# Two pieces of work change places in a software-pipelined attention layer: the block sums of the norms on TensorE, the sums of squares on GpSimd

## The chip, the cores and the metric

The kernel runs on one core of one Trainium2 chip. The metric is the device time of one execution in microseconds (us). Profiled times come from one execution that the hardware profiler recorded. The core has five engines with a queue each: TensorE (PE, with its weight loads shown apart as PEld), VectorE (DVE), ScalarE (ACT), GpSimd (POOL) and SyncE (SP), which here only issues DMAs. Each engine runs its queue strictly in order; between engines only semaphores order the work.

## The reference

The input x is 8 x 256 x 128. It is layer-normalised; then two branches are added to it. The first is causal attention with 16 heads of 64. The second is six layers of local attention and an MLP, and nearly all of the time is spent there:

```
for i in range(DEPTH):                                  # DEPTH = 6
    x = attn_layer(shift_tokens(x), ...) + x
    x = ffn_layer(shift_tokens(x), ...) + x

qkv = x @ Wqkv
q = l2norm(q) * qs ; k = l2norm(k) * ksc                # norm over the 64 elements of a head
q = q * cos * scale + rotate_half(q) * sin * scale      # k likewise, with 1 / scale
sim = q k^T * 8 in windows of 32 queries and 64 keys, softmax, times v, then @ Wo

a, gate = split(layernorm(x) @ W1 + b1)
out = a * gelu(gate) @ W2 + b2
```

## The kernel before

A *unit* is one batch element in one layer (6 x 8 = 48 units), a *group* is four heads of it, so there are 192 groups. After the causal branch the kernel runs a stream of *slots*; slot s works on five groups at different stages. Every engine has its own function `slot(s)`, and the statements in it are that engine's queue: the order is written out by hand, and the scheduler of the hardware changes nothing in it.

What a slot s does, along the chain of one group m:

- TensorE projects k and q of group s+4 in high and low parts (L789 to L791, `project`) and v (L799 to L801, `values`) into the banks B_K, B_Q and B_N.
- VectorE multiplies k and q with the rotary tables (L1025, L1026, `rotate`); ScalarE squares them (L520, `squares`); GpSimd adds the two halves of the rotated vectors (L395, `rotated`) and the two halves of the squares (L415, tile `sqs`).
- TensorE adds up `sqs` over the 32 rows of each head with a matrix of ones (L833, `con("blk")`, into B_N, semaphore `n_done`): these are the **block sums of the norms**. ScalarE turns them into 1/norm with Ln and Exp (L556, L559), VectorE bounds that (L1066, `bound_ready`), and GpSimd multiplies it into k and then q (L409, tile `z_norm`, `zn_ready`): the **normalisations**. SP copies the result into `zqk` with eight DMAs (L325). All of this is for group s+3.
- TensorE computes the scores of group s (L749, L758, `windows`), VectorE and ScalarE do the softmax (L1004, L1006, L552, L1011 to L1016).
- For group s-1 TensorE turns the probabilities (L768, `turn_windows`, into B_T, `turned`), ScalarE spreads them out (L539, `spread_ready`), TensorE multiplies them with V (L780, `weigh_windows`, 64 rows wide, into B_T again, `lpv_done`), and ScalarE copies the product to `yt` (L583, `lyt_ready`). `turn_windows` of the next slot waits for `lyt_ready`, since it writes B_T.
- For group s-2 TensorE multiplies `yt` with Wo (L828).
- In seven of eight slots there is also a piece of the MLP or of its layer norm: the gate product (L850, copied by ScalarE at L589), the up product (L864, taken by VectorE at L1085), the down product (L872), the centring (L886) and the mean of squares (L894) at the end of TensorE's slot. They all use the one bank B_M, so L886 and L894 wait for `gate_ready` or `hid_ready`, that is, until L589 or L1085 of the same slot has read it.

ScalarE's queue in a slot is: copy of v (L531), spreading (L539), in every fourth slot the layer norm's Ln and Exp (L546, L549), Exp of the scores (L552), Ln and Exp of the norms (L556, L559), squares of k (L520), the square or the scaling of the layer norm (L574 or L578), the copy to `yt` (L583), the gate (L589), once in eight slots the Gelu with its two table loads (L593, L595, L599, L542), squares of q (L520).

GpSimd's queue in a slot is: rotated k (two of L395), both normalisations (two of L409), sums of squares (L415), rotated q (two of L395); at the turn of a layer the split of the weights (L386, L388).

TensorE's queue in a slot, where the change is (before):

```
if two:
    pe.wait_ge(S["lv_ready"], s + 4)
    pe.wait_ge(S["sums_ready"], s + 4)
    pe.matmul(B_N[:, :], con("blk"), sqs...).then_inc(S["n_done"], 1)
if four:
    weigh_windows(s - 1, ...)
```

Of the kernel before, what the change touches and what calls it, by code (L numbers as in the profile page):

```python
# [11 lines left out]
ALU = mybir.AluOpType  # L12
# [4 lines left out]
P = 128  # L17
NB, T = 8, 256
# [3 lines left out]
G, HG = 4, 4  # L22
# [82 lines left out]
def build(nc, x, w_kv_down, w_kv_up, w_q, w_out, Wqkv, q_scale, k_scale, Wo, ln_g, ln_b, W1, b1, W2, b2, const, out):  # L105
    with ExitStack() as ctx:  # L106
        def sb(name, shape, dt=F32):
            return ctx.enter_context(nc.sbuf_tensor(name, shape, dt))

        def sem(name):  # L110
            return ctx.enter_context(nc.semaphore(name))
# [3 lines left out]
        def con(name):  # L115
            at, n = CONST[name]
            return consts[:, at:at + n]
# [32 lines left out]
        z_raw = sb("z_raw", [P, 2, 2, 2, T])  # L150
        z_norm = sb("z_norm", [P, 2, 2, 2, T])
# [14 lines left out]
        rinv = probs_t.rearrange("p h c -> p (h c)")[:, 2 * GW * 2:].rearrange("p (a t) -> p a t", a=2)  # L166
# [30 lines left out]
        S = {n: sem(n) for n in names}  # L197
# [3 lines left out]
        def after(eng, name, value):  # L201

            if not (isinstance(value, int) and value <= 0):
                eng.wait_ge(S[name], value)
# [31 lines left out]
        def stream(slot):  # L236

            for s in range(FIRST, LAST):
                slot(s)

        def active(s, first, last):

            return first <= s < last
# [5 lines left out]
        def layer_begun(s, at):  # L249

            l, k = divmod(s - at, LAYER)
            return l + 1 if k == 0 and 0 <= l < DEPTH - 1 else 0
# [118 lines left out]
        @block.gpsimd  # L371
        def _(pool):
            pool.memset(tiny[:, 0:1], 2.0 ** -64).then_inc(S["tiny_ready"], 1)
            pool.wait_ge(S["tiny_ready"], 1)
            pool.memset(tiny[:, 1:2], EPS).then_inc(S["tiny_ready"], 1)
            pool.wait_ge(S["tiny_ready"], 2)
            pool.memset(xs[64:P, :, 0:1], 0.0).then_inc(S["zeros_ready"], 1)
            pool.wait_ge(S["zeros_ready"], 1)
            pool.memset(par_rows[:, :], 0.0).then_inc(S["zeros_ready"], 1)

            pool.memset(v_late[0:WIN, :, 0, :], 0.0).then_inc(S["spread_zero"], 1)

            def split_weights(l, g):

                cols = slice(g * GW, (g + 1) * GW)
                pool.tensor_copy(w_high[:, :, cols], w_qkv[:, :, cols]).then_inc(S["split_high"], 1)  # L386
                pool.wait_ge(S["split_high"], G * l + g + 1)
                pool.tensor_tensor(w_low[:, :, cols], w_qkv[:, :, cols], w_high[:, :, cols].bitcast(F32), ALU.subtract).then_inc(S["split_done"], 1)  # L388

            def rotated(m, parity, idx, prod, mark):  # L390

                pool.wait_ge(S[prod], m + 1)
                after(pool, "zn_ready", m - 1)
                for half in range(2):
                    a = pool.tensor_tensor(z_raw[:, parity, idx, half, :], rot_u[:, idx, half, :], rot_v[:, idx, 1 - half, :], ALU.add)  # L395
                a.then_inc(S[mark], 1)

            def slot(s):
                one, two = active(s, -4, GROUPS - 4), active(s, -3, GROUPS - 3)
                if one:  # L400
                    rotated(s + 4, s % 2, 1, "k_prod", "k_summed")
                if two:

                    m, parity = s + 3, (s + 3) % 2
                    pool.wait_ge(S["bound_ready"], m + 1)
                    after(pool, f"z_in{(s + 1) % G}", 16 * 2 * HG * ((s + 1) // G + 1))
                    for idx, summed in ((1, "k_summed"), (0, "q_summed")):
                        pool.wait_ge(S[summed], m + 1)
                        a = pool.tensor_tensor(z_norm[:, parity, idx, :, :], rinv[:, idx, :].unsqueeze(1).broadcast_to([P, 2, T]), z_raw[:, parity, idx, :, :], ALU.mult)  # L409
                    a.then_inc(S["zn_ready"], 1)  # L410
                if one:
                    pool.wait_ge(S["k_square"], s + 5)
                    pool.wait_ge(S["q_square"], s + 5)
                    after(pool, "n_done", s + 4)
                    pool.tensor_tensor(sqs[:, :, :], sq[:, :, 0, :], sq[:, :, 1, :], ALU.add).then_inc(S["sums_ready"], 1)  # L415
                    rotated(s + 4, s % 2, 0, "q_prod", "q_summed")
                for g in range(G):
                    l = layer_begun(s, LAYER - 7 + g)
                    if l:
                        pool.wait_ge(S["w_in"], 16 * 3 * (l + 1))  # L420
                        pool.wait_ge(S["lv_done"], s + 4)
                        split_weights(l, g)

            pool.wait_ge(S["pv_done"], STEPS)
            pool.memset(spread[:, :, :, :], 0.0).then_inc(S["spread_zero"], 1)  # L425
            pool.wait_ge(S["w_in"], 16 * 3)
            for g in range(G):
                split_weights(0, g)
            stream(slot)

        @block.scalar
# [189 lines left out]
        def _(pe):  # L621
# [5 lines left out]
            for p in range(PAIRS):  # L627
                for k in range(2 * TT):
                    m = pe.transpose(bank[p][:, k * P:(k + 1) * P], xn_rows[:, 2 * TT * p + k, :], ident)
# [141 lines left out]
            def weigh_windows(n, unit, g, odd):  # L771

                pe.wait_ge(S["lv_ready"], n + 1)
                pe.wait_ge(S[f"v_late_in{g}"], 32 * (unit + 1))
                pe.wait_ge(S["spread_ready"], n + 1)
                for pair, tile, a in itertools.product(range(2), range(TILES), range(2)):
                    h, t = 2 * pair + a, tile // 2
                    f = slice(g * GW + h * D, g * GW + (h + 1) * D)
                    y = B_T[D * a:D * a + D, T * pair:T * pair + T].rearrange("p (t x s c) -> p t s x c", t=TT, x=2, s=2)
                    mm = pe.matmul(y[:, t, tile % 2, :, :], (v_sb if tile % 2 else v_late)[:, odd, t, f], spread[:, h, tile, :], start=True, stop=True,  # L780
                                   tile_position=(0, D * a), skip_group_check=True)
                mm.then_inc(S["lpv_done"], 1)
# [21 lines left out]
            def slot(s):  # L804
                g = s % G
                one, two = active(s, -4, GROUPS - 4), active(s, -3, GROUPS - 3)
                four = active(s, 1, GROUPS + 1)
# [11 lines left out]
                if active(s, 2, GROUPS + 2):  # L819

                    n, og, unit = s - 2, (s - 2) % G, (s - 2) // G
                    pe.wait_ge(S["lyt_ready"], n + 1)
                    if (s - 2) % LAYER < G:
                        pe.wait_ge(S[f"wo_in{og}"], 16 * ((s - 2) // LAYER + 1))
                    if og == 0:
                        after(pe, "lres_done", unit)
                    for c in (2 * og, 2 * og + 1):
                        mm = pe.matmul(B_X[:, 0:T], wo[:, c, :], yt[:, c, :], start=(c == 0), stop=(c == HD // P - 1))  # L828
                    mm.then_inc(S["lwo_done"], 1)
                if two:  # L830
                    pe.wait_ge(S["lv_ready"], s + 4)
                    pe.wait_ge(S["sums_ready"], s + 4)
                    pe.matmul(B_N[:, :], con("blk"), sqs[:, :, :].rearrange("p a t -> p (a t)"), start=True, stop=True).then_inc(S["n_done"], 1)  # L833
                if four:
                    weigh_windows(s - 1, (s - 1) // G, (s - 1) % G, (s - 1) // G % 2)
                for c in range(3):
                    if mlp_slot(s, 13 + c):
                        p = (s - 13 - c) // (2 * G)
# [67 lines left out]
            for h in range(HG):  # L906
                pt_taken(STEPS - 1, h)
            stream(slot)
            for p in range(PAIRS):
                pe.wait_ge(S["fin_sum"], p + 1)  # L910
                for k in range(2 * TT):
                    m = pe.transpose(bank[p][:, k * P:(k + 1) * P], xh[:, 2 * p + k // 2, (k % 2) * P:(k % 2 + 1) * P], ident)
# [225 lines left out]
```

## Time and profile before

| | us |
|---|---|
| median of 3 runs | 2024.2 |
| lowest, highest | 2021.36, 2025.51 |
| profiled execution, its own time | 2020.56 |
| its span in the profile | 2018.7 |
| granted TensorE clock, mean | 0.99 of full speed |

The span runs from the first to the last instruction of the program. Busy time of an engine is time in which it executes; an engine that waits for a semaphore is idle, and a row then names in brackets how long it sat and who released it. Matmuls are pipelined, so one row's end lies slightly behind the next row's start; distances are best taken from start to start. A slot is counted here from the start of `turn_windows` (L768) to the next one. The stream repeats itself every eight slots (two units), to within some hundredths of a microsecond; slot 0 to slot 7 below are the eight of one such group of eight, beginning with a slot whose number is divisible by eight.

### The profile page before, as it was taken

How to read it: one execution, taken by the hardware profiler on the slowest of the kernel's cores; microseconds unless marked ns; L12 is line 12 of the kernel's file. 1: busy time of each engine (PE TensorE's matmuls, PEld its weight loads, DVE VectorE, ACT ScalarE, POOL GpSimd, SP SyncE). 2: the span in 40 equal slices, each digit the busy share in tenths (PEclk: the TensorE clock that was granted, in tenths of full speed). 3: DMA queues.
4: the chain of work that ended last, by engine and by line, in shares of the span. 5: the costliest groups of instructions: out<-in, count | busy, mean ns of one | idle time of the engine just before them, and what ended most of it. 6: DMA issues, size and time to landing. Idle time of an engine off the chain costs nothing. (4 is left out here: it accounts for less than half of the span.)

```text
span 2018.7 us, 68336 instructions
## 1 busy us (share of the span) xinstructions
PE 1892.6 (94%) x26905; PEld 1389.3 (69%) x26905; DVE 1573.9 (78%) x3055; ACT 1407.2 (70%) x2840; POOL 1340.6 (66%) x1402
## 2 busy tenths in 40 slices
PE   4999997799999999999999999999999999999995
PEld 3677665677767777767777677776777776777762
DVE  5666665688888788888888888888878888888773
ACT  2666565578677767777777777768777777777762
POOL 0000002898898787897787987779878889787740
PEclk9999999999999999999999999999999999999996
DMA  3000000344434334333344343343333433333330
GB/s 97 2 1 0 0 6 30 97 108 106 124 86 104 96 100 127 87 95 97 99 113 111 85 105 95 100 124 88 100 97 99 128 88 94 97 99 101 93 92 21
DMA packets 190580, 171.18 MB, mean 85 GB/s; under 512 B 32160, under 2 KB 186440, under 8 KB 190152
## 3 DMA queue, kind: packets, MB, share of 16 engines
q1 hardware_dynamic: 190280, 167.02, 31.6%
q8 instruction: 208, 3.41, 0.7%
q14 instruction: 92, 0.75, 0.1%
HBM read 21.14 MB, written 1.05 MB: 11 GB/s over the span
## 5 line engine op out<-in xcount | busy, mean ns | idle before, releaser
L395 POOL TENSOR_TENSOR z_raw<-rot_u,rot_v 128x256 f32<-128x256 f32 x768 | 551.7, 741 | 151.9 <-DVE rot_v L1026 150.0
L409 POOL TENSOR_TENSOR z_norm<-probs_t,z_raw 128x512 f32<-128x512 f32 x384 | 492.7, 1304 | 97.5 <-DVE probs_t L1066 97.5
L1025 DVE TENSOR_TENSOR rot_u<-bank,tabs 128x512 f32<-128x512 f32 x384 | 262.7, 684 | 183.9 <-ACT sq L520 179.9
L789 PE MATMUL bank<-x_high,w_high 128*128 128x256 f32 x768 | 302.9, 394 | 2.3 <-issue 1.1
L1026 DVE TENSOR_TENSOR rot_v<-bank,tabs 128x512 f32<-128x512 f32 x384 | 260.9, 680 | 0.0
L552 ACT ACTIVATE pair_bank<-pair_bank 128x512 f32<-128x512 f32 x192 | 111.7, 582 | 211.3 <-DVE pair_bank L1006 211.0
L415 POOL TENSOR_TENSOR sqs<-sq 128x512 f32<-128x512 f32 x192 | 244.9, 1276 | 20.4 <-POOL z_norm L409 20.4
L520 ACT ACTIVATE sq<-bank 128x512 f32<-128x512 f32 x384 | 225.1, 588 | 47.8 <-PE bank L791 44.5
L780 PEld LDWEIGHTS bank<-probs_t,v_late 128*64 128x64 f32 x3072 | 155.2, 137 | 144.5 <-issue 144.5
L833 PE MATMUL bank<-sqs,consts 128*128 128x512 f32 x384 | 203.9, 613 | 52.5 <-POOL sqs L415 48.8
L539 ACT ACTIVATE probs_t<-bank 64x512 f32<-64x512 f32 x384 | 226.6, 590 | 33.8 <-PE bank L768 31.5
L425 POOL MEMSET probs_t<- 128x1024 f32 x1 | 1.0, 961 | 334.8 <-PE bank L690 334.8
L790 PE MATMUL bank<-x_high,w_low 128*128 128x256 f32 x768 | 216.5, 282 | 0.0
L791 PE MATMUL bank<-x_low,w_high 128*128 128x256 f32 x768 | 216.4, 282 | 0.0
L556 ACT ACTIVATE probs<-bank,tiny 128x512 f32<-128x512 f32 x192 | 131.9, 687 | 112.5 <-PE bank L833 111.5
L780 PE MATMUL bank<-probs_t,v_late 128*64 128x64 f32 x3072 | 199.1, 228 | 0.5 <-ACT probs_t L539 0.5
L828 PE MATMUL bank<-yt,wo 128*128 128x256 f32 x768 | 197.7, 380 | 1.3 <-ACT yt L583 1.3
L780 PE MATMUL bank<-probs_t,v_sb 128*64 128x64 f32 x3072 | 190.0, 222 | 0.0
L789 PEld LDWEIGHTS bank<-x_high,w_high 128*128 128x128 f32 x768 | 145.1, 189 | 62.2 <-issue 42.8
L790 PEld LDWEIGHTS bank<-x_high,w_low 128*128 128x128 f32 x768 | 145.7, 190 | 37.9 <-issue 37.9
L1004 DVE TENSOR_REDUCE nm<-pair_bank 128x8 f32<-128x512 f32 x192 | 131.9, 687 | 43.0 <-PE pair_bank L758 40.5
L758 PE MATMUL pair_bank<-zqk 64*32 64x64 f32 (+1 forms) x12288 | 162.2, 221 | 0.0
(154 smaller groups left out, 4507.9 us busy)
## 6 DMA issues: line engine op xcount, KB each, us to landing
zqk<-z_norm SPq DMA_DIRECT2D x1536, 64.0 KB, 2.1
v_late<-v_sb SPq DMA_DIRECT2D x192, 192.0 KB, 2.6
w_qkv<-in_L_ffn_Wqkv SPq DMA_DIRECT2D x18, 512.0 KB, 5.2
v_late<-v_sb SPq DMA_DIRECT2D x192, 32.0 KB, 2.2
wo<-in_L_ffn_Wo SPq DMA_DIRECT2D x24, 128.0 KB, 2.4
w<-in_L_ffn_W SPq DMA_DIRECT2D x12, 170.5 KB, 2.9
consts<-in_constants SPq DMA_DIRECT2D x1, 1088.0 KB, 5.2
w_qkv<-in_L_attn_w_kv_up SPq DMA_DIRECT2D x2, 512.0 KB, 6.3
```

What stands on the lines that cost most here:

```text
L395: a = pool.tensor_tensor(z_raw[:, parity, idx, half, :], rot_u[:, idx, half, :], rot_v[:, idx, 1 - half, :], ALU.add)
L409: a = pool.tensor_tensor(z_norm[:, parity, idx, :, :], rinv[:, idx, :].unsqueeze(1).broadcast_to([P, 2, T]), z_raw[:, parity, idx, :, :], ...
L415: pool.tensor_tensor(sqs[:, :, :], sq[:, :, 0, :], sq[:, :, 1, :], ALU.add).then_inc(S["sums_ready"], 1)
L520: act.activation(sq[:, idx, :, :], src[:, :].rearrange("p (a t) -> p a t", a=2), ACT.Square).then_inc(S[mark], 1)
L539: a = act.activation(spread[rows, :, :, WIN * x:WIN * x + WIN], tiles[rows, :, :, :], ACT.Copy)
L780: mm = pe.matmul(y[:, t, tile % 2, :, :], (v_sb if tile % 2 else v_late)[:, odd, t, f], spread[:, h, tile, :], start=True, stop=True, tile ...
L789: pe.matmul(dst, w_high[:, j, cols], x_high[:, odd, :], start=True, stop=False)
L790: pe.matmul(dst, w_low[:, j, cols], x_high[:, odd, :], start=False, stop=False)
L791: mm = pe.matmul(dst, w_high[:, j, cols], x_low[:, odd, :], start=False, stop=True)
L833: pe.matmul(B_N[:, :], con("blk"), sqs[:, :, :].rearrange("p a t -> p (a t)"), start=True, stop=True).then_inc(S["n_done"], 1)
L1025: dve.tensor_tensor(rot_u[:, idx, :, :], src, tabs[:, 2 * idx, :, :], ALU.mult)
L1026: dve.tensor_tensor(rot_v[:, idx, :, :], src, tabs[:, 2 * idx + 1, :, :], ALU.mult).then_inc(S[mark], 1)
```

## The change

On TensorE `weigh_windows` of group s-1 is issued in front of the block sums instead of behind them. On GpSimd the sums of squares are issued between the normalisation of k and that of q instead of behind both. Nothing is added or taken away.

```
@@ gpsimd
+            def normalise(parity, idx):
+
+                return pool.tensor_tensor(z_norm[:, parity, idx, :, :], rinv[:, idx, :].unsqueeze(1).broadcast_to([P, 2, T]), z_raw[:, parity, idx, :, :], ALU.mult)
...
                 if two:
 
-                    m, parity = s + 3, (s + 3) % 2
-                    pool.wait_ge(S["bound_ready"], m + 1)
+                    pool.wait_ge(S["bound_ready"], s + 4)
                     after(pool, f"z_in{(s + 1) % G}", 16 * 2 * HG * ((s + 1) // G + 1))
-                    for idx, summed in ((1, "k_summed"), (0, "q_summed")):
-                        pool.wait_ge(S[summed], m + 1)
-                        a = pool.tensor_tensor(z_norm[:, parity, idx, :, :], rinv[:, idx, :].unsqueeze(1).broadcast_to([P, 2, T]), z_raw[:, parity, idx, :, :], ALU.mult)
-                    a.then_inc(S["zn_ready"], 1)
+                    pool.wait_ge(S["k_summed"], s + 4)
+                    normalise((s + 3) % 2, 1)
                 if one:
                     pool.wait_ge(S["k_square"], s + 5)
                     pool.wait_ge(S["q_square"], s + 5)
                     after(pool, "n_done", s + 4)
                     pool.tensor_tensor(sqs[:, :, :], sq[:, :, 0, :], sq[:, :, 1, :], ALU.add).then_inc(S["sums_ready"], 1)
+                if two:
+                    pool.wait_ge(S["q_summed"], s + 4)
+                    normalise((s + 3) % 2, 0).then_inc(S["zn_ready"], 1)
+                if one:
                     rotated(s + 4, s % 2, 0, "q_prod", "q_summed")
@@ tensor
+                if four:
+                    weigh_windows(s - 1, (s - 1) // G, (s - 1) % G, (s - 1) // G % 2)
                 if two:
                     pe.wait_ge(S["lv_ready"], s + 4)
                     pe.wait_ge(S["sums_ready"], s + 4)
                     pe.matmul(B_N[:, :], con("blk"), sqs[:, :, :].rearrange("p a t -> p (a t)"), start=True, stop=True).then_inc(S["n_done"], 1)
-                if four:
-                    weigh_windows(s - 1, (s - 1) // G, (s - 1) % G, (s - 1) // G % 2)
```

TensorE's queue in a slot 2, before: the output product, the block sums, the products with V (their first three rows), the MLP's product, then, further on, the values, the centring and the next slot's turning.

```order
L828 MATMUL bank<-yt,wo 128x256
L833 MATMUL bank<-sqs,consts 128x512 [waits sums_ready,lv_ready]
L780 MATMUL bank<-probs_t,v_late 64x2x32 [waits spread_ready,v_late_in1,lv_ready]
L780 MATMUL bank<-probs_t,v_late 64x2x32
L780 MATMUL bank<-probs_t,v_sb 64x2x32 x2
...
L864 MATMUL bank<-xh,w 128x512 [waits hid_ready]
...
L799 MATMUL bank<-w_high,x_high 128x256 [waits ln_done]
...
L886 MATMUL bank<-xs,consts 128x256 [waits hid_ready,ln_var,lres_done]
L768 MATMUL bank<-consts,probs 128x128 [waits lyt_ready,weights_ready]
```

The same place of the changed kernel (its line numbers are 5 to 7 higher here):

```order
L833 MATMUL bank<-yt,wo 128x256
L785 MATMUL bank<-probs_t,v_late 64x2x32 [waits spread_ready,v_late_in1,lv_ready]
L785 MATMUL bank<-probs_t,v_late 64x2x32
L785 MATMUL bank<-probs_t,v_sb 64x2x32 x2
...
L840 MATMUL bank<-sqs,consts 128x512 [waits sums_ready,lv_ready]
L869 MATMUL bank<-xh,w 128x512 [waits hid_ready]
...
L804 MATMUL bank<-w_high,x_high 128x256 [waits ln_done]
...
L891 MATMUL bank<-xs,consts 128x256 [waits hid_ready,ln_var,lres_done]
L773 MATMUL bank<-consts,probs 128x128 [waits lyt_ready,weights_ready]
```

The block sums moved behind all sixteen products with V; each kept its waits, and what follows them stayed where it was.

GpSimd's queue in one slot, before: rotated k, the normalisations of k and q, the sums of squares, rotated q.

```order
L395 TENSOR_TENSOR z_raw<-rot_u,rot_v 128x256 [waits zn_ready,k_prod]
L409 TENSOR_TENSOR z_norm<-probs_t,z_raw 128x512 [waits k_summed,z_in0,bound_ready]
L409 TENSOR_TENSOR z_norm<-probs_t,z_raw 128x512 [waits q_summed]
L415 TENSOR_TENSOR sqs<-sq 128x512 [waits n_done,q_square,k_square]
L395 TENSOR_TENSOR z_raw<-rot_u,rot_v 128x256 [waits zn_ready,q_prod]
```

And in the changed kernel:

```order
L399 TENSOR_TENSOR z_raw<-rot_u,rot_v 128x256 [waits zn_ready,k_prod]
L392 TENSOR_TENSOR z_norm<-probs_t,z_raw 128x512 [waits k_summed,z_in0,bound_ready]
L416 TENSOR_TENSOR sqs<-sq 128x512 [waits n_done,q_square,k_square]
L392 TENSOR_TENSOR z_norm<-probs_t,z_raw 128x512 [waits q_summed]
L399 TENSOR_TENSOR z_raw<-rot_u,rot_v 128x256 [waits zn_ready,q_prod]
```

The sums of squares, with their wait for ScalarE's squares, now stand in front of the normalisation of q.

## Rows read from the trace of the kernel before

**Rows 1.** The page: span, and TensorE's busy time, share and instructions.

```profile
span 2018.7 us, 68336 instructions
PE 1892.6 (94%) x26905; PEld 1389.3 (69%) x26905; DVE 1573.9 (78%) x3055; ACT 1407.2 (70%) x2840; POOL 1340.6 (66%) x1402
```

**Rows 2.** Waits, whole span: who waited for whom; us in total, times, longest.

```profile
ACT probs L556 <- PE bank L833: 111.5, 148, 7.1
PE bank L833 <- POOL sqs L415: 48.8, 55, 4.9
PE bank L768 <- ACT yt L583: 12.5, 46, 0.3
```

**Rows 3.** Busy time by stretch: slots 0 to 7 but 4, from L768 to L768.

```profile
962.86:970.06 7.20, 6.92 (x127) 5.50 (x126) 6.59 (x13) 5.87 (x12) 5.58 (x7) 1.00 0.40 102
970.06:979.24 9.18, 8.05 (x129) 5.84 (x129) 7.06 (x13) 9.07 (x14) 6.53 (x8) 1.00 0.49 126
979.24:987.66 8.42, 8.31 (x130) 6.17 (x131) 7.60 (x14) 5.62 (x12) 7.80 (x9) 1.00 0.28 70
987.66:995.67 8.01, 8.01 (x131) 6.14 (x130) 6.77 (x13) 5.62 (x11) 6.69 (x8) 1.00 0.44 112
...
1005.00:1012.62 7.62, 7.62 (x130) 5.90 (x129) 7.35 (x13) 5.00 (x10) 4.28 (x6) 1.00 0.39 101
1012.62:1021.27 8.65, 8.29 (x132) 6.14 (x131) 6.51 (x13) 6.45 (x13) 8.22 (x9) 1.00 0.29 70
1021.27:1029.37 8.10, 8.10 (x131) 6.21 (x130) 5.84 (x12) 5.95 (x12) 6.43 (x8) 1.00 0.42 109
```

**Rows 4.** The same view: eight slots at a layer's turn, eight slots early on.

```profile
1095.87:1166.43 70.56, 65.97 (x1035) 48.38 (x1034) 58.74 (x98) 52.97 (x98) 63.73 (x65) 1.00 0.35 89
428.78:489.17 60.39, 59.66 (x1024) 46.48 (x1023) 51.41 (x93) 45.51 (x85) 53.96 (x58) 1.00 0.42 108
```

**Rows 5.** Timeline of TensorE: start, us, line, operands, [idle before, releaser].

```profile
966.05 1.02 PE L833 MATMUL bank<-sqs,consts 128*128 128x512 f32 x2
967.00 0.34 PE L780 MATMUL bank<-probs_t,v_late 128*64 128x64 f32 x4
...
968.08 0.39 PE L789 MATMUL bank<-x_high,w_high 128*128 128x256 f32 x1
...
970.06 0.63 PE L768 MATMUL bank<-consts,probs 128*128 128x128 f32 x4 [0.28 <-ACT yt L583]
...
974.32 1.10 PE L833 MATMUL bank<-sqs,consts 128*128 128x512 f32 x2 [0.88 <-POOL sqs L415]
```

**Rows 6.** Timeline of TensorE at a layer's turn, in a slot 6.

```profile
1153.40 1.10 PE L833 MATMUL bank<-sqs,consts 128*128 128x512 f32 x2 [1.44 <-POOL sqs L415]
```

**Rows 7.** Timeline of ScalarE in slots 0, 1, 5 and 7.

```profile
967.11 0.69 ACT L556 ACTIVATE probs<-bank,tiny 128x512 f32<-128x512 f32 x1 [0.59 <-PE bank L833]
...
969.33 0.58 ACT L583 ACTIVATE yt<-bank 128x512 f32<-128x512 f32 x1
...
973.67 1.18 ACT L539 ACTIVATE probs_t<-bank 64x512 f32<-64x512 f32 x2
...
976.77 0.69 ACT L556 ACTIVATE probs<-bank,tiny 128x512 f32<-128x512 f32 x1
...
1009.93 0.69 ACT L556 ACTIVATE probs<-bank,tiny 128x512 f32<-128x512 f32 x1
...
1011.66 0.59 ACT L583 ACTIVATE yt<-bank 128x512 f32<-128x512 f32 x1
...
1028.04 0.68 ACT L589 ACTIVATE gate<-bank,gate_bias 85x512 f32<-85x512 f32 x1
```

**Rows 8.** Timeline of VectorE in slot 3: the up product's taking.

```profile
994.02 0.75 DVE L1085 SCALAR_TENSOR_TENSOR hid<-bank,out_bias,gate 85x512 f32<-85x512 f32 x1 [0.22 <-PE bank L864]
```

**Rows 9.** Timeline of GpSimd at the start of slot 1: sums of squares.

```profile
972.90 1.27 POOL L415 TENSOR_TENSOR sqs<-sq 128x512 f32<-128x512 f32 x1 [0.81 <-POOL z_norm L409]
```

**Rows 10.** The page's DMA issues: count, KB each, us from issue to landing.

```profile
zqk<-z_norm SPq DMA_DIRECT2D x1536, 64.0 KB, 2.1
```

## The prediction

> **What bounds the kernel now.** I read the page first: TensorE is busy for 94% of the span [rows 1], so at first sight only its own gaps count. The waits show one large gap there: TensorE waited 48.8 us, in 55 places, for GpSimd's sums of squares in front of the block sums, and ScalarE waited 111.5 us, in 148 slots of 192, for the block sums themselves [rows 2]. Then I cut the stream into slots. They repeat to 0.02 us, so one group of eight can be worked. Its lengths are 7.20, 9.18, 8.42, 8.01, 9.33 (slot 4, between the bounds of its neighbours), 7.62, 8.65 and 8.10 us, in all 66.51 [rows 3]. Last I read the timelines. They show a **loop**: TensorE turns the probabilities (962.86), comes to the block sums 3.19 us later (966.05) [rows 3, 5]; ScalarE, idle for 0.59 us, starts Ln at 967.11 and, after Exp, the squares of k and the scaling of the layer norm, ends its copy to `yt` at 969.91 [rows 7]; 0.15 us later TensorE may turn again, at 970.06, having sat idle for it [rows 5]. So the two shortest steps of TensorE in a slot are tied to the block sums through ScalarE's queue, though the copy needs nothing of them. TensorE's 94% does not show this: those waits are short (12.5 us in 46 places [rows 2]) because the loop and TensorE's own work are nearly equally long now.
>
> **The move on TensorE.** From start to start the block sums take 0.95 us (966.05 to 967.00) and the products with V 1.08 us (967.00 to 968.08) [rows 5]. The change swaps them: what follows both stays where it is, the products end 0.95 us earlier, the block sums 1.08 us later. The earlier products gain nothing: the copy of them to `yt` stands behind Ln and Exp of the norms in ScalarE's queue. The later block sums cost wherever ScalarE had waited for them. Behind the waiting Ln are queued Exp, the squares of k, the layer norm's step, the copy to `yt`, the gate and the squares of q. The price of an entry of the sums behind 64-column products is not in the trace: the lower bound of the delay is 1.08 us; the upper is 1.17, if the roughly 0.1 us by which the products' step exceeds the sums' is spent on entering and the sums pay it too. I take 1.08, since the sums' row behind other full-width products is the nearest, and keep 1.17 for the range.
>
> What this does slot by slot (Ln now starts 5.33 us after the turn at the earliest, where it was 4.25):
>
> - Slot 0: Ln waits, the copy follows in the queue, TensorE already waits for it: the whole 1.08. **+1.08**.
> - Slot 1: here TensorE waited 0.88 us for the sums of squares and started them at 974.32 [rows 5]. The products may now start, but they need the spreading, which ScalarE, held up by the Gelu, ends at 974.85 [rows 7]. So they start at about 975.00, the sums at 976.08, and end some 1.06 later at 977.14; Ln started at 976.77 [rows 7], now about 977.13. **+0.36**.
> - Slot 2: TensorE gains some 0.3 us of a wait for squares, but the centring (L886) waits for L1085, which VectorE does behind L1066, and that needs the norms. **0**.
> - Slot 3: L1085 ran from 994.02 to 994.77 [rows 8]. L1066 in front of it now waits for Exp, 0.7 us past that, and L894 starts 0.15 behind L1085: **+0.36** after the slack it had.
> - Slot 4: TensorE's own work, 9.33, is over the loop's 8.28. **0**.
> - Slot 5: Ln started at 1009.93, 4.93 after the turn, and the copy ended at 1012.25, 2.32 later [rows 7]. Now 5.33 + 2.32 + 0.15 = 7.80 against 7.62 [rows 3]. **+0.18**.
> - Slot 6: TensorE gains 0.53 us of a wait for squares, but the gate copy (L589) ends at 8.23 after the turn and L886 waits for it: 8.80 against 8.65. **+0.15**.
> - Slot 7: the mean of squares (L894) waits for the gate copy, which ended at 1028.72 [rows 7], 0.65 us before the next turn. **+1.08**.
>
> The sum is 3.2 us in 66.5, with the removed waits already taken off.
>
> **The move on GpSimd.** Four instructions of a slot keep their times; only their order changes. The sums of squares come up to 1.3 us earlier, but not before ScalarE's squares of q: in slot 1 they start at 972.90 after an idle 0.81 us behind the normalisations [rows 9], and cannot come earlier there. That wait now stands in front of the normalisation of q, with rotated q queued behind it. I cost this at nothing in an ordinary group: GpSimd is busy for 5.6 to 8.2 us of a slot [rows 3] and has idle time before the next rotated k. The normalised q comes up to 2.4 us later (1.1 from the norms, 1.3 from the squares). Its readers are the eight DMAs of a slot, 2.1 us each to land [rows 10], and the scores two slots further on; no wait of TensorE for them is among the waits. If that cover were gone the delay would be paid once, not in every slot, as no queue in front of GpSimd waits for the scores: 2.4 us.
>
> **The sum.** Sixteen ordinary groups of eight: 16 x 3.2 = 51. Five groups at a layer's turn (70.56 us [rows 4]), where GpSimd also splits weights: the wait of 1.44 us for the squares in their slot 6 [rows 6] goes, and that slot ends at 8.80 where it took 9.73; slot 5 gives 0.2; but slots 0 and 7 pay 1.08 each, slot 1 0.36, and slots 3 and 4, long with ScalarE's rotary tables, 0.4 and 0.2: +2.0 each, 10 together. The first two groups have little MLP, so slots were 7.05 to 7.5 us (60.39 in eight [rows 4]) and the loop's floor is now 7.80, 8.10 or 8.28 by what ScalarE has in it: +10. The last group, half of it without projections: +2. In all **+73 us**, or 2020.6 + 73 = 2094 against the profiled execution's own time. That execution lies 3.6 us under the median of the runs shown, so against the median I forecast **2097 us**, 3.6% slower. About 0.2%, 4 us, is what a measurement here can tell from no change.
>
> **The rivals.**
>
> *The gap closes.* If ScalarE's queue had slack for 1.08 us, the change would do what the waits suggest: the sums of squares are early enough, TensorE's 48.8 us [rows 2] go, and the time is about 2024 - 49 = 1975. For it speaks that every one of these waits is on the busiest engine. Against it: the idle 0.28 us of TensorE directly for the copy in slot 0 [rows 5], which means no slack at all there, and the 0.15 us between gate copy and L894 in slot 7. Chance 0.10. The Trainium skill, in Perfetto Trace Analysis, section Optimization Strategy, says to find the gaps on the engine that binds and to make what ends them come sooner. By that rule the change is right; the trace agrees that the gap is there, but shows a second path with equal length beside it.
>
> *Half of it.* The delay reaches TensorE only where it now waits with no slack, slots 0 and 7 (2.16 us a group), and the 1.9 us of waits in slots 1, 2 and 6 are gained in full, because L1085 and the gate copy are not as late as I work out. Then a group costs 0.3 us net: 21 x 0.3 + 10 for the first groups, less 5 x 1 at the turns of layers: about 2035. Chance 0.07.
>
> *It evens out.* The same with the spreading in slot 1 earlier too: within 4 us of 2024. That the reordering does nothing, because GpSimd's squares are late anyway and TensorE waits behind the products as before, would come to more than this, not to nothing, as Ln is later still. Chance 0.04.
>
> *More than I work out.* The sums pay 0.1 us on entry as well: 0.1 x 7 slots x 24 groups = 17 us more, 2114. This is a bound of my forecast, not another mechanism.
>
> **How the numbers follow.** My forecast, with its bounds from 2080 (some of the slacks in slots 1, 3, 5 and 6 larger: 24 x 0.7 us less) to 2114, has 0.79; half 0.07, even 0.04, gap closes 0.10. The range of 2062 to 2116 holds the forecast with a margin for the groups that I worked less closely, and leaves out the rest, about 0.2. Slower by over 0.2%: 0.79 + 0.07 = 0.86; within 0.2%: 0.04; faster: 0.10.
>
> **What would show it.** Right: the wait of TensorE for `sqs` nearly gone; ScalarE's wait for the block sums up from 111.5 us towards 200 or more; TensorE's waits for the copy to `yt` up from 12.5 us to some tens, and new waits in front of L886 and L894 for the gate copy and L1085; slots 0 and 7 at 8.3 and 9.2 us, slot 1 at 9.5, slot 4 unchanged at 9.33; in slot 1 a wait of the products for the spreading; granted clock still 1.00 in the middle of the stream, as in all of [rows 3]. Wrong: slot 0 still at 7.2 us (no loop through ScalarE), or slots 3 and 6 shorter than before (the guards of the bank B_M do not bind), or TensorE waiting for the normalised q (the move on GpSimd costs).

## The result and the profile after

The changed kernel takes **2132.4 us** (median of 5 runs, 2129.99 to 2133.73) where the kernel before, measured beside it, takes 2024.2 (2021.36 to 2026.11): a ratio of 1.054, interval 1.052 to 1.055. It is 108 us slower, where 73 were forecast with a range that ended at 2116. Sign and mechanism were right, the size was not.

The page of the changed kernel:

```profile
span 2128.2 us, 68336 instructions
PE 1911.0 (90%) x26905; PEld 1405.5 (66%) x26905; DVE 1569.3 (74%) x3055; ACT 1394.5 (66%) x2840; POOL 1331.4 (63%) x1402
```

The instructions are the same in number, and their busy time changes by 18 us on TensorE [rows 1]; the rest of the 109.5 us of span is waiting. Its waits over the whole span (who waited for whom, us in total, times, longest):

```profile
ACT probs L561 <- PE bank L840: 286.3, 191, 7.1
...
DVE probs_t L1071 <- ACT probs_t L564: 139.4, 169, 3.4
...
PE bank L773 <- ACT yt L588: 47.7, 81, 1.2
...
PE bank L785 <- ACT probs_t L544: 34.4, 23, 1.6
...
PE bank L899 <- ACT gate L594: 25.0, 23, 1.1
...
PE bank L891 <- ACT gate L594: 18.6, 23, 0.9
PE bank L899 <- ACT xc L579: 10.3, 7, 1.9
PE bank L891 <- DVE hid L1090: 9.8, 23, 0.9
PE bank L840 <- POOL sqs L416: 9.5, 5, 4.9
...
PE bank L899 <- DVE hid L1090: 7.2, 18, 0.9
```

The change did what it says: TensorE's wait for the sums of squares fell from 48.8 us to 9.5 [rows 2]. In its place ScalarE waits 286.3 us for the block sums, not 111.5, and hands that on: to VectorE (139.4, behind Exp), and to TensorE for the copy (47.7), the spreading (34.4) and the gate copies (25.0 and 18.6), 126 us in all where these four had 15 before, nearly all of it the copy [rows 2]. The same two matmuls, centring (L891) and mean of squares (L899), wait for the up product's taking (9.8 and 7.2) and for the square of `xc` (10.3) as well, 27 us where they had 7. The slots of one ordinary group of eight (columns as in [rows 3]; the last stretch is a slot 4 at a layer's turn):

```profile
1005.12:1013.61 8.49, 7.18 (x128) 5.56 (x126) 7.09 (x13) 5.88 (x12) 6.45 (x7) 1.00 0.29 76
1013.61:1023.26 9.65, 7.88 (x129) 5.94 (x129) 6.91 (x13) 9.07 (x14) 6.02 (x8) 1.00 0.32 80
1023.26:1031.95 8.69, 8.32 (x130) 6.32 (x131) 7.40 (x14) 5.52 (x12) 7.18 (x9) 1.00 0.41 104
1031.95:1040.63 8.68, 8.31 (x132) 6.24 (x131) 6.49 (x12) 5.27 (x11) 6.52 (x8) 1.00 0.38 96
1040.63:1049.96 9.33, 9.33 (x133) 6.65 (x132) 7.74 (x13) 6.44 (x12) 6.73 (x8) 1.00 0.35 90
1049.96:1057.96 8.00, 7.77 (x131) 5.88 (x129) 7.72 (x14) 4.77 (x10) 5.87 (x7) 1.00 0.30 78
1057.96:1067.07 9.11, 8.30 (x130) 6.31 (x131) 5.95 (x12) 6.56 (x13) 7.27 (x9) 1.00 0.44 108
1067.07:1076.45 9.38, 8.28 (x131) 6.21 (x130) 6.12 (x12) 5.91 (x12) 6.57 (x8) 1.00 0.45 117
1184.96:1196.42 11.46, 10.89 (x133) 7.70 (x133) 7.92 (x13) 7.99 (x17) 9.64 (x10) 0.85 0.32 84
```

The group is 71.33 us, 4.8 more than [rows 3]. Every slot but slot 4 has grown, and in all of them but slot 4 TensorE's busy time is under the slot's length. TensorE's timeline in slots 0 and 1 and at the ends of slots 2, 3 and 7 shows where (start, us, [idle before, releaser]):

```profile
1007.45 1.03 PE L833 MATMUL bank<-yt,wo 128*128 128x256 f32 x4
1008.41 0.34 PE L785 MATMUL bank<-probs_t,v_late 128*64 128x64 f32 x4
...
1009.49 1.13 PE L840 MATMUL bank<-sqs,consts 128*128 128x512 f32 x2
...
1013.61 0.63 PE L773 MATMUL bank<-consts,probs 128*128 128x128 f32 x4 [1.24 <-ACT yt L588]
...
1018.54 0.34 PE L785 MATMUL bank<-probs_t,v_late 128*64 128x64 f32 x4 [1.55 <-ACT probs_t L544]
...
1031.44 0.67 PE L891 MATMUL bank<-xs,consts 128*128 128x256 f32 x2 [0.37 <-DVE hid L1090]
...
1040.12 0.67 PE L899 MATMUL bank<-xc,consts 128*128 128x256 f32 x2 [0.37 <-DVE hid L1090]
...
1075.94 0.67 PE L899 MATMUL bank<-xc,consts 128*128 128x256 f32 x2 [1.10 <-ACT gate L594]
```

And ScalarE's in slot 0:

```profile
1010.65 0.69 ACT L561 ACTIVATE probs<-bank,tiny 128x512 f32<-128x512 f32 x1 [1.87 <-PE bank L840]
...
1012.88 0.58 ACT L588 ACTIVATE yt<-bank 128x512 f32<-128x512 f32 x1
```

Ln starts 5.53 us after the turn (1010.65 less 1005.12); before it was 4.25 (967.11 less 962.86, [rows 3, 7]). The delay of the norms is 1.28 us, and TensorE's wait for the copy grew from 0.28 us to 1.24: the loop of the prediction, longer than it was worked out.

### The profile page after: what moved, and what is told of

It reads as the page before. It is cut to its first block and busy times, and to the rows that moved or that the text cites. A ratio compares the mean times of both kernels' runs of the same rounds, so it can differ in the third digit from the quotient of the medians.

```text
span 2128.2 us, 68336 instructions
## 1 busy us (share of the span) xinstructions
PE 1911.0 (90%) x26905; PEld 1405.5 (66%) x26905; DVE 1569.3 (74%) x3055; ACT 1394.5 (66%) x2840; POOL 1331.4 (63%) x1402
## 5 line engine op out<-in xcount | busy, mean ns | idle before, releaser
L561 ACT ACTIVATE probs<-bank,tiny 128x512 f32<-128x512 f32 x192 | 132.0, 688 | 286.3 <-PE bank L840 286.3
L794 PE MATMUL bank<-x_high,w_high 128*128 128x256 f32 x768 | 314.5, 409 | 1.9 <-issue 1.1
L785 PE MATMUL bank<-probs_t,v_late 128*64 128x64 f32 x3072 | 198.8, 228 | 34.4 <-ACT probs_t L544 34.4
L840 PE MATMUL bank<-sqs,consts 128*128 128x512 f32 x384 | 218.6, 652 | 9.5 <-POOL sqs L416 9.5
L1071 DVE TENSOR_SCALAR probs_t<-probs_t 128x512 f32<-128x512 f32 x192 | 89.0, 463 | 139.4 <-ACT probs_t L564 139.4
```

The source lines that it names most:

```text
L794: pe.matmul(dst, w_high[:, j, cols], x_high[:, odd, :], start=True, stop=False)
```

## The experiments

Nine kernels ran, each several times beside the kernel before. Slot lengths below are those of an ordinary group of eight, from the start of one turning to the next.

### One half of the change at a time

The block sums behind the products, GpSimd as before:

```
+                if four:
+                    weigh_windows(s - 1, (s - 1) // G, (s - 1) % G, (s - 1) // G % 2)
                 if two:
...
-                if four:
-                    weigh_windows(s - 1, (s - 1) // G, (s - 1) % G, (s - 1) // G % 2)
```

> The move on TensorE alone (block sums behind the products with V); GpSimd's order as before. Theory A (the loss comes from the later block sums, through ScalarE's queue): the same as the changed kernel in ordinary slots, as the sums of squares end by 3.6 us after the turn and the block sums start only at 4.37; at the turns of layers slot 6 waits up to 0.3 us for them: 2130 to 2137 us. Theory B (the move on GpSimd, with the normalisation of q queued behind the wait for ScalarE's squares, causes the 35 us that the forecast lacks): 2090 to 2100 us.

Measured: 2132.83 us, ratio 1.055 (1.053 to 1.057), a group 71.3: the whole of the change.

And the change's part for GpSimd, word for word, with TensorE as before; its core:

```
-                    for idx, summed in ((1, "k_summed"), (0, "q_summed")):
...
+                    normalise((s + 3) % 2, 1)
...
                     pool.tensor_tensor(sqs[:, :, :], sq[:, :, 0, :], sq[:, :, 1, :], ALU.add).then_inc(S["sums_ready"], 1)
+                if two:
+                    pool.wait_ge(S["q_summed"], s + 4)
+                    normalise((s + 3) % 2, 0).then_inc(S["zn_ready"], 1)
```

> The move on GpSimd alone (sums of squares between the normalisations); TensorE's order as before. Theory A: TensorE's wait for the sums of squares goes in slots 2 and 6 (0.3 and 0.5 us) and at the turns of layers (1.4 us and some), while slot 1 keeps its 0.9 us, since ScalarE's squares of q end that one: about 0.8 x 24 + 8 = 27 us less, 1997 us, and never over 2024. Theory B: at or over 2024, up to 2060 us.

Measured: 1998.87 us, ratio 0.989 (0.986 to 0.992). Slots 2 and 6 of its stream:

```profile
973.09:981.15 8.06, 8.06 (x130) 6.24 (x131) 7.52 (x14) 5.62 (x12) 7.43 (x9) 1.00 0.41 104
...
1006.25:1014.30 8.05, 8.05 (x132) 6.23 (x131) 6.60 (x13) 6.45 (x13) 7.69 (x9) 1.00 0.44 110
```

They were 8.42 and 8.65 [rows 3]; now TensorE has no idle time in them. 0.36 and 0.60 in sixteen ordinary groups are 15 us, the five groups at a layer's turn are 1.2 us shorter each (69.4 instead of 70.6), which is 6 more, and 23 were gained. So the halves don't add: the GpSimd half is worth 23 us alone and nothing beside the other, since sums that start 1.2 us later find their squares ready in any case.

### The copy taken out of ScalarE's queue behind the norms

The changed kernel, with the copy to `yt` in front of Ln instead of behind the squares of k and the layer norm's step:

```
+                if four:
+                    og = (s - 1) % G
+                    act.wait_ge(S["lpv_done"], s)
+                    after(act, "lwo_done", s - G)
+                    act.activation(yt[:, 2 * og:2 * og + 2, :], B_T.rearrange("p (c t) -> p c t", c=2), ACT.Copy).then_inc(S["lyt_ready"], 1)
...
-                if four:
-                    og = (s - 1) % G
...
```

> The changed kernel, and in ScalarE's queue the copy to yt (waits only for the products) moved in front of Ln of the norms, so that the next turn no longer hangs on the block sums. Theory A: the part of the loss that runs through the copy goes: slots 0 and 1 together 17.3 instead of 18.1, slot 5 7.62 instead of 8.00, slots 6 and 7 0.5 shorter each since the gate stands one copy earlier, slots 2 and 3 unchanged (8.69, 8.68) since L1090 hangs on Exp of the norms: 2.2 us in 71.4, with the early slots some 65 us, about 2067 us. Rival C (the turn is not held by the copy but by softmax or TensorE's own extra work after the swap): within 10 us of 2132.

Measured: 2087.23 us, ratio 1.033 (1.030 to 1.036), so 45 of the 108 us come back, 20 fewer than expected. Slot 0 is 7.09 and slots 0 and 1 together 17.27, as worked out: TensorE does wait through ScalarE's queue. Some 13 of the 20 us that are missing are in slot 1, two of which are shown:

```profile
991.20:1001.38 10.18, 7.70 (x130) 5.93 (x129) 7.90 (x14) 10.05 (x16) 6.70 (x8) 1.00 0.33 86
1060.26:1072.06 11.80, 9.32 (x130) 6.68 (x129) 8.38 (x15) 10.44 (x16) 7.20 (x8) 0.86 0.30 76
```

In 8 of 22 groups the granted clock of this slot is 0.86 and it is 1.6 to 1.7 us longer. In all 22 the products wait about 2.48 us for the spreading, where they wait 1.55 in the changed kernel; in those 8 the block sums behind that wait take 2.08 us instead of 1.12:

```profile
1066.10 0.34 PE L785 MATMUL bank<-probs_t,v_late 128*64 128x64 f32 x4 [2.48 <-ACT probs_t L544]
...
1067.37 2.08 PE L840 MATMUL bank<-sqs,consts 128*128 128x512 f32 x2
```

### The price of the block sums' new neighbours

To see what the 0.2 us over the forecast's 1.08 are, the changed kernel ran with the products in front of the output product too, so that this one stands directly behind them and the sums behind a full-width product again:

```
+                if four:
+                    weigh_windows(s - 1, (s - 1) // G, (s - 1) % G, (s - 1) // G % 2)
...
                     mm.then_inc(S["lwo_done"], 1)
-                if four:
-                    weigh_windows(s - 1, (s - 1) // G, (s - 1) % G, (s - 1) // G % 2)
```

> The changed kernel with the products with V put in front of the output product, so the block sums are as late in the slot as in the changed kernel but follow a full-width matmul whose weights can be loaded ahead. Theory D (0.2 us of the 1.28 us delay is the price of entering the block sums behind the 64-column products, half of it the second weight load): the block sums end at 5.39 instead of 5.49 after the turn, 0.1 us in seven of eight slots: about 2115 us. Rival: the delay is set by what stands in front, whatever the order: 2132 us, within 3.

Measured: 2177.68 us, ratio 1.076 (1.073 to 1.078), which neither theory had. The ordinary slots are those of the changed kernel (8.47, 8.68, 9.38), and the price has only moved to the output product:

```profile
1027.35 1.13 PE L835 MATMUL bank<-yt,wo 128*128 128x256 f32 x4
1028.32 1.02 PE L840 MATMUL bank<-sqs,consts 128*128 128x512 f32 x2
```

The output product takes 1.13 us here, 1.03 in the changed kernel; the sums 1.02 here, 1.13 there. Whatever stands directly behind the 64-column products takes 0.1 us longer, and whatever stands in front takes as much longer to hand over: the sums start 0.95 us ahead of the products [rows 5], and only 0.86 ahead of a full-width product, as in slot 0 of a version that comes below:

```profile
955.82 1.02 PE L827 MATMUL bank<-sqs,consts 128*128 128x512 f32 x2
956.68 1.02 PE L837 MATMUL bank<-yt,wo 128*128 128x256 f32 x4
```

Of the 48 us that the profiled execution is longer than that of the changed kernel, 39 are in slot 1, which takes 10.51 us in ten groups and 11.84 to 13.13 in the other twelve, instead of 9.65, and 5 are in slot 6 (9.27 instead of 9.11). In slot 1 the output product now queues behind products that wait 2.4 us for the spreading, and in those twelve groups the granted clock is down behind that wait.

The weight loads show what goes with a switch. First the changed kernel, then the kernel before:

```profile
1009.49 0.30 PEld L840 LDWEIGHTS bank<-sqs,consts 128*128 128x128 f32 x2
```

```profile
965.84 0.41 PEld L833 LDWEIGHTS bank<-sqs,consts 128*128 128x128 f32 x2
...
967.00 0.20 PEld L780 LDWEIGHTS bank<-probs_t,v_late 128*64 128x64 f32 x4 [0.76 <-issue]
```

Behind the output product the sums' weights are loaded 0.21 us before their matmul (965.84, 966.05); at either edge of the products load and matmul start together (1009.49 twice, 967.00 twice). The Trainium skill, in TensorE: Matmul & The Clock Gate, section Part 2: What happens when you issue a matmul, says that the engine pulls a weight load ahead of running matmuls where row groups don't conflict or the background buffer takes it. The rows agree inside each kind of product (among the products with V a load at 967.11 stands before its matmul at 967.17). At the edge between the two kinds they show no load ahead, and 0.1 us more; that the one causes the other is not shown.

The other way to a shorter delay is the sums amid the products, behind the first eight of sixteen:

```
+                    if (pair, tile, a) == (1, 0, 0):
+                        between()
...
+                    weigh_windows(s - 1, (s - 1) // G, (s - 1) % G, (s - 1) // G % 2, block_sums)
```

> The changed kernel with the block sums issued after eight of the sixteen products with V. Half a dose of the delay: block sums end at about 4.9 after the turn (0.1 to enter the products, 0.54 for eight, 0.1 to leave). Theory A: slots 0 and 7 are in proportion (7.9 and 8.8 us), slots 2, 3 and 5 have enough slack and stay at 8.07, 8.01 and 7.62, slot 6 at 8.5: about 2 us over e2 in 66, 2050 to 2060 us. If the loss were a fixed price of the products ahead of the sums, not of the time: 2120 to 2132 us.

Measured: 2082.13 us, ratio 1.030 (1.027 to 1.032). That is over the 2050 to 2060 expected. Ln starts 5.07 us after the turn, 0.82 of the 1.28 us of delay, and slot 0 takes 8.03 us, 0.83 of the 1.29 us of loss (7.9 was expected); slot 7 takes 8.9 to 9.06 (8.8 expected). So the dependence on the delay holds in between too. The rest is a second pair of edges, which lengthens TensorE's own work. Slot 4, 9.33 us both before and in the changed kernel, takes 9.70 here, and TensorE never idles in it:

```profile
1020.38:1030.08 9.70, 9.70 (x134) 6.67 (x133) 7.57 (x13) 6.33 (x12) 6.64 (x7) 1.00 0.40 102
```

```profile
989.81 1.12 PE L841 MATMUL bank<-sqs,consts 128*128 128x512 f32 x2
990.86 0.34 PE L787 MATMUL bank<-probs_t,v_late 128*64 128x64 f32 x4
```

So leaving the products and entering them once more costs about 0.36 us, not 0.2: 0.1 is in the longer first matmul behind them and 0.1 in the later start of the next run of products, and the rest is inside the products, where the first and the last step of a run take 0.17 and 0.22 us and those between 0.12.

### All three paths cut

On top of the copy in front, the gate copy (L594) directly behind Exp on ScalarE, and the taking of the up product (L1090) in front of the clipped exponentials (L1071) on VectorE; here ScalarE's edit:

```
+                for c in range(3):
+                    if mlp_slot(s, 13 + c):
...
+                        act.activation(gate[0:CW[c], c, :], B_M[0:CW[c], :], ACT.Identity, bias=gate_bias[0:CW[c], c:c + 1]).then_inc(S["gate_ready"], 1)
                 if four:
...
-                for c in range(3):
-                    if mlp_slot(s, 13 + c):
...
```

> The changed kernel with TensorE and GpSimd untouched, and three things taken out from behind Ln and Exp of the norms: the copy to yt in front of Ln (as e3), the gate copy directly behind Exp, and on VectorE the up product's taking (L1090) in front of the bound of the norms (L1071). Theory A: then nothing that TensorE waits for stands behind the block sums; slots 2 to 7 are at TensorE's own 8.07, 8.01, 9.34, 7.61, 8.05, 8.10, slots 0 and 1 as in e3 (7.09, 10.18): 66.5 for eight as before the change, about 2026 us. If other waits on the norms hold TensorE (the values' wait for Ln, the normalised q): over 2060 us.

Measured: 2057.6 us, ratio 1.016 (1.014 to 1.019), between the two. Slots 2, 5 and 6 are at 8.04, 7.61 and 8.11, no longer than in the kernel before. Slot 3 (8.26) and slot 7 (8.83) are not: L899 now waits for the square of `xc` (L590), in front of which the gate copy now stands. Here slot 7:

```profile
1043.84 0.70 PE L899 MATMUL bank<-xc,consts 128*128 128x256 f32 x2 [0.52 <-ACT xc L590]
```

A queue that is late makes something late, whichever step goes first. Slot 1 takes 10.17, and 11.6 to 13.1 in 12 of 22 groups, with the granted clock down again.

### The opposite direction

If a delay of the block sums costs, less of it should gain. GpSimd's order as changed, and the block sums in front of the output product, except in slot 1 of eight, where their squares are late:

```
+                if two and s % 8 != 1:
+                    pe.wait_ge(S["lv_ready"], s + 4)
+                    pe.wait_ge(S["sums_ready"], s + 4)
+                    pe.matmul(B_N[:, :], con("blk"), sqs[:, :, :].rearrange("p a t -> p (a t)"), start=True, stop=True).then_inc(S["n_done"], 1)
...
                     mm.then_inc(S["lwo_done"], 1)
-                if two:
+                if two and s % 8 == 1:
                     pe.wait_ge(S["lv_ready"], s + 4)
```

> Squares early on GpSimd (as e2), and the block sums moved the other way on TensorE: in front of the output product (L828 of before), 0.86 us earlier, except in slot 1 of eight, where the sums of squares come late. Theory A (loop through ScalarE's queue) with the sign turned: Ln of the norms starts at 3.7 after the turn instead of 4.25 (the scores' Exp is then what holds it), slot 0 falls from 7.20 to TensorE's own 6.76, the early slots without MLP to 6.8 too, slot 1 by 0.1, the rest is TensorE's own work and stays: 0.5 x 24 + 4 = 16 us under e2, about 1983 us. If slot 0 were held by something else (softmax, the projections): the same as e2, 1999 us.

Measured: 1991.2 us, ratio 0.984 (0.982 to 0.986), 8 us under the version with early squares alone, where 16 were expected. Slots 0, 6 and 7:

```profile
953.49:960.25 6.76, 6.76 (x128) 5.51 (x127) 5.98 (x13) 6.08 (x12) 5.44 (x7) 1.00 0.36 95
...
1002.24:1010.53 8.29, 8.29 (x132) 6.33 (x131) 6.59 (x13) 6.61 (x13) 7.83 (x9) 1.00 0.40 101
1010.53:1018.53 8.00, 8.00 (x131) 6.14 (x130) 6.01 (x12) 6.25 (x12) 6.61 (x8) 1.00 0.46 122
```

Slot 0 went from 7.20 [rows 3] to 6.76, the figure expected, and TensorE is busy for all of it: there the loop through ScalarE is off the path. Slot 6 is 8.29, 0.24 over the version with early squares alone. The groups at a layer's turn gain nothing (69.3 to 69.5 us in both): their slot 4 takes 10.5 us where it took 9.36. The next kernel has the sums behind the output product in slot 6 as well:

```
-                if two and s % 8 != 1:
+                if two and s % 8 not in (1, 6):
...
-                if two and s % 8 == 1:
+                if two and s % 8 in (1, 6):
```

> The squares early, and the block sums in front of the output product's step in slots 0, 2, 3, 4, 5 and 7 of eight, behind it in slots 1 and 6. In the kernel with the sums in front everywhere but in slot 1, slot 6 took 8.29 us, where the squares early alone gave 8.05: read as TensorE waiting there for the sums of squares with the output product queued behind. If that is the cause, slot 6 comes back to 8.05, a group to 64.9, and the time is 22 x 0.24 = 5 us less, about 1986. If slot 6 stays near 8.29 or its neighbours lengthen by as much, the 0.24 us belongs to the loop through ScalarE, and the time stays at 1991.

Measured: 1986.72 us, ratio 0.983 (0.981 to 0.984), slot 6 at 8.05 and a group at 64.8, as expected. It is the best of all versions, 1.7% or 35 us under the kernel before that ran beside it (2021.56). Its lead over the version without this edit is within the spread of their times; slot 6 shows it, 8.05 for 8.29 in the ordinary groups and 8.9 for 9.7 at a layer's turn.

Last, slot 1, the longest one: the squares of q in front of the Gelu, and in slot 1 the copy between Ln and Exp, on top of the version with the sums in front:

```
+                    if four and s % 8 == 1:
+                        copy_product(s)
...
+                if one:
+                    squares(s + 4, "lq_done", B_Q, 0, "q_square")
...
-                if one:
-                    squares(s + 4, "lq_done", B_Q, 0, "q_square")
```

> e5, and in ScalarE's queue the squares of q in front of the Gelu (slot 0 of eight), so that slot 1's sums of squares are early, and in slot 1 the copy to yt between Ln and Exp of the norms, since there ScalarE itself is late. Slot 1 is then held by TensorE's own work behind the spreading, about 8.3 instead of 9.1 us: 20 us under e5, about 1963 us. If slot 1 is held by ScalarE's total (9.07 us busy of 9.18), slot 2 gives back what slot 1 gains: same as e5.

Measured: 1995.28 us, ratio 0.986 (0.985 to 0.987), no gain: the second of the two cases. Slots 1 and 2:

```profile
961.06:969.40 8.34, 7.98 (x130) 5.80 (x129) 6.71 (x11) 8.24 (x13) 6.64 (x7) 1.00 0.46 113
969.40:978.38 8.98, 8.35 (x132) 6.35 (x131) 8.42 (x16) 6.23 (x13) 7.84 (x9) 1.00 0.36 91
```

Slot 1 came down from 8.95 us to the 8.3 expected, and slot 2 gave 0.9 back: ScalarE, busy for all but 0.1 us of slot 1, owes its work in slot 2 instead.

## Why the prediction was right in kind and short in size

**What held.** The path: the copy stands in ScalarE's queue behind norms that it doesn't need. Taking it out gave 45 us back, and slot 0 follows the start of Ln: with Ln at 4.25, 5.07 and 5.53 us after the turn (before, sums amid the products, behind them) it is 7.20, 8.03 and 8.49; with Ln at 3.58 it is 6.76, TensorE's own work. Slot 4, TensorE's own work, stayed at 9.33. In slot 1 the products wait for the spreading; L891 and L899 wait for gate copy and L1090. The granted clock is 1.00 in the ordinary groups. The GpSimd move, costed at nothing, costs nothing. "The gap closes" fell although its premise was true: the 48.8 us were real, and about half of them are to be had by the GpSimd half alone, with nothing put in ScalarE's way. "Half of it" fell as well: none of the gates that it took for slack was slack.

**The step that failed** is the first term, "I take 1.08 ... and keep 1.17 for the range". It measured 1.28: 0.10 on entering the 64-column products, 1.08 for them, 0.10 on leaving, which the sums pay as the first full-width product behind them. The upper bound counted one edge, and the prediction held that no row had its price. Both could be read before: the 0.95 from sums to products [rows 5] already holds the entry, and the trace of before has edges of the other kind. The first projection behind the products takes 0.39 us (968.08, [rows 5]), the next on the same line 0.28 (968.54), and the up product directly behind the products takes 1.12 us where the sums took 1.02 [rows 5]:

```profile
984.84 1.12 PE L864 MATMUL bank<-xh,w 128*128 128x512 f32 x2
```

Slot by slot, forecast and measured increase in us:

```
slot        0     1     2     3     4     5     6     7    sum
forecast  1.08  0.36  0     0.36  0     0.18  0.15  1.08   3.2
measured  1.29  0.47  0.27  0.67  0     0.38  0.46  1.28   4.8
```

The 0.2 us is there in each slot but 1 and 4. Slots 2, 3 and 6 have some 0.1 more: there Ln starts 5.55 to 5.57 us after the turn, not 5.53, and I had read the chain behind it too short by the rest. In slots 2 and 3 that is Exp, L1071, L1090, 0.15 us, then L891 or L899. In slot 6 it is the gate copy, which ends 8.46 us after the turn (forecast 8.23), and the 0.65 us from there to the next turn (forecast 0.57).

Over the run: sixteen ordinary groups 78 us (forecast 51), five groups at a layer's turn 19.4 (10), the first two 11.4 (10), the last 2.5 (2), before these groups and behind the last turning -1.5; in all 109.5. Of the 36 us missed, 27 are the ordinary groups and so mostly that one term. At a layer's turn slots 3 and 4 grew by 0.58 and 0.40, where 0.4 and 0.2 were worked out, and two of the five slots 4 took 11.46 instead of 10.11 with the granted clock at 0.85 (last row of the stretches above), 2.7 us together, which the prediction had no case for. Why it fell in these two and not in the other three stays open.

**The range** was too narrow for the same reason: its upper end was built from a bound on the delay that was itself taken for certain.

## What to carry to other kernels

Before a step is moved back on the busiest engine to let a wait pass, look at who waits for its result and at what is queued behind that waiter: here 39 us of TensorE's waits closed and about 130 us of others opened, because ScalarE works in the order of its queue and its copy was behind the norms. Pull the late input forward instead (GpSimd's order alone: 23 us gained), and move the step forward where its input allows. And price a moved step at both its new edges, by the rows of whatever stands at such an edge now.

## What the runs showed that was not expected

- At each switch of TensorE between 64-column and full-width products 0.1 us is paid outside the products, independently of what stands at the edge: the sums 1.13 against 1.02, the output product 1.13 against 1.03, the start of the products 0.95 against 0.86 us behind the start of the sums. At neither edge are weights loaded ahead. One more round trip costs TensorE 0.36 us in all (slot 4 with the sums amid the products, 9.70 against 9.33), while moving the sums from one side of the products to the other left TensorE's own work as it was (slot 4 at 9.33 in both).
- In some groups the granted clock fell to half directly behind an idle time of TensorE (block sums of 1.12 us then took 2.08), and the slot became 1.2 to 1.7 us longer, in two cases 2.6 and 3.0. Behind an idle time of 2.48 us in slot 1 it fell in 8 of 22 groups with the copy first and in 12 of 22 with all three cuts; behind 2.42 us, in 12 of 22 with the products in front. Behind 1.88 us, at the end of slot 3 at a layer's turn, it fell in two of five turns of the changed kernel, in one or two of five in three other versions and in all five with all three cuts. Behind the 1.55 us in slot 1 of the changed kernel it never fell. In the kernel before and in the three fastest versions no idle time of TensorE in these 22 groups was over 1.5 us, and the clock stayed at 1.00. Groups with the same idle time differ, so what decides between them stays open.
